# Expert bias rows and their selector as 128-row matmul operands instead of 40-row ones

## What is computed

```python
xf = _layernorm(x.reshape(-1, Dd), ln_g, ln_b)
logits = xf @ router_w
scores, idx = jax.lax.top_k(logits, K)          # K = 2 of E = 8 experts
gate = jax.nn.softmax(scores, axis=-1)
# one expert:
x = _layernorm(x, g, b)
x1 = x @ W1 + b1
x2 = jnp.clip(x @ W2 + b2, -20.0, 20.0)
hidden = jnp.clip(x1 * (x2 * jax.nn.sigmoid(x2)), -10000.0, 10000.0)
return jnp.clip(hidden @ Wo + bo, -10000.0, 10000.0)
```

## Time and profile before

| | |
|---|---|
| median of 3 runs | 579.73 us |
| lowest, highest | 577.4 us, 579.78 us |
| span of the profiled execution | 574.8 us |
| mean granted TensorE clock | 0.954 of full speed |
| instructions | 6831 |
| TensorE matmuls, VectorE, ScalarE, GpSimd instructions | 2579, 669, 406, 143 |

### The profile page before, as it was taken

The page is one execution under the profiler, slowest core; times in us unless marked ns, Lnnn a source line. Parts: engine busy times, 40 slices in busy tenths (PEclk is TensorE's granted clock), DMA queues, the critical chain, the costliest instruction groups (busy, mean ns, idle before and its releaser), DMA issues.

```text
span 574.8 us, 6831 instructions
## 1 busy us (share of the span) xinstructions
PE 514.5 (89%) x2579; PEld 444.6 (77%) x2579; DVE 430.0 (75%) x669; ACT 280.2 (49%) x406; POOL 234.6 (41%) x143
## 2 busy tenths in 40 slices
PE   3899999999999998989988886579999999996994
PEld 3899889999999997878877674456777676674773
DVE  6558977734433345889997776866999999997996
ACT  3425313332332235767775013329669659647630
POOL 5000433333333411122226712323686696690762
PEclk9999999999999999889999979569999999998889
DMA  8289763343344331020016233574888988984632
GB/s 315 94 282 343 234 260 121 121 146 98 125 147 146 128 137 70 1 74 1 1 58 210 114 111 109 196 285 175 328 322 310 388 313 324 391 298 180 220 110 111
DMA packets 20929, 106.32 MB, mean 185 GB/s; under 512 B 4720, under 2 KB 5104, under 8 KB 11168
## 3 DMA queue, kind: packets, MB, share of 16 engines
q1 hardware_dynamic: 15328, 91.53, 42.7%
q0 software_dynamic: 3696, 7.96, 4.2%
q10 hardware_dynamic: 1872, 6.39, 3.6%
HBM read 98.96 MB, written 6.91 MB: 184 GB/s over the span
## 4 chain that ended last, share of the span: by engine, by line
PE 52%; DVE 28%; issue 8%; ACT 5%; POOL 4%; DMA 1%; DVEq 0%; ACTq 0%; POOLq 0%
PE ps L1115 46%; DVE lo L728 11%; DVE sg L1031 4%; PE ps L1178 3%; POOL xres L480 2%; PE ps L1218 1%; ACT hi L561 1%; DVE xres L1047 1%; ACT xg L645 1%; DVE y L1001 1%; DVE hh L1038 1%; DVE x2c L1027 1%; DVE xg_lo L988 1%; DVE ht_lo L993 1%; ACT sg L654 1%
## 5 line engine op out<-in xcount | busy, mean ns | idle before, releaser
L728 DVE TENSOR_TENSOR lo<-raw,hi 128x2048 fp32r<-128x2048 f32 x58 | 153.8, 2668 | 54.8 <-ACT hi L561 54.6
L561 ACT ACTIVATE hi<-raw 128x2048 fp32r<-128x2048 f32 x70 | 131.8, 1913 | 77.0 <-PE ps L1115 65.0
L447 POOL DMA_INDIRECT mask_rows<-colf,bits x48 | 55.9, 1164 | 134.7 <-DMA mask_rows<-colf,bits 82.1
L489 POOL TENSOR_TENSOR lo<-raw,hi 128x2048 fp32r<-128x2048 f32 x12 | 64.9, 5408 | 50.5 <-ACT hi L561 50.4
L1115 PE MATMUL ps<-xt_hi,hi 128*128 128x384 f32 x192 | 65.2, 340 | 2.2 <-DVE xt_lo L744 2.2
L1115 PE MATMUL ps<-xt_lo,hi 128*128 128x384 f32 x192 | 65.1, 339 | 0.0
L1115 PE MATMUL ps<-xt_hi,lo 128*128 128x384 f32 x192 | 64.9, 338 | 0.0
L1115 PE MATMUL ps<-hi,xg_hi 128*128 128x512 f32 x128 | 54.3, 425 | 7.2 <-DVE lo L728 5.7
L1115 PE MATMUL ps<-lo,xg_hi 128*128 128x512 f32 x128 | 52.3, 409 | 0.0
L1115 PE MATMUL ps<-hi,xg_lo 128*128 128x512 f32 x128 | 52.2, 408 | 0.0
L455 POOL TENSOR_SCALAR pr<-pr,small 128x384 f32<-128x384 f32 x16 | 19.9, 1246 | 75.0 <-DVE small L853 75.0
(11 more groups left out here) (209 smaller groups left out, 1131.1 us busy)
## 6 DMA issues: line engine op xcount, KB each, us to landing
raw<-in_wf SPq DMA_DIRECT2D x42, 1024.0 KB, 6.3
raw<-in_wg SPq DMA_DIRECT2D x28, 1024.0 KB, 5.5
xfb<-in_wf SPq DMA_DIRECT2D x6, 1024.0 KB, 5.8
src_i<-in_srcb ACTq DMA_DIRECT2D x4, 768.0 KB, 6.2
dst_i<-in_dstb ACTq DMA_DIRECT2D x4, 768.0 KB, 9.0
y_rows<-y SPq DMA_DIRECT2D x6, 512.0 KB, 2.9
xin<-in_x SPq DMA_DIRECT2D x3, 512.0 KB, 4.4
xres<-in_x SPq DMA_DIRECT2D x3, 512.0 KB, 4.2
```

The source lines that it names most:

```text
L447: pool.indirect_dma_start(out=mbuf[:, :], out_offset=bass.IndirectOffsetOnAxis(ap=bits[:, 1, g:g + 1], axis=0), in_=colf[:, 5, g:g + 1], i ...
L489: pool.tensor_tensor(lo[SLOT[c]][:, :], raws[RAW[c]], f32(hi[SLOT[c]][:, :]), ALU.subtract).then_inc(pool_lo_done, 1)
L561: act.activation(hi[SLOT[c]][:, :], raws[RAW[c]], ACT.Copy).then_inc(hi_done, 1)
L728: dve.tensor_tensor(lo[SLOT[c]][:, :], raws[RAW[c]], f32(hi[SLOT[c]][:, :]), ALU.subtract).then_inc(lo_done, 1)
```

## The change

`brow_f`, `brow`, `sels` and `selx` get 128 rows in place of 48. The clearing of `brow_f` and `sels`, the rounding of `brow_f` into `brow` and the setting of `selx` run over 128 rows. The bias matmuls read all 128 rows of both operands. Rows 48 to 127 are zero. The loads, the low parts in rows 32 to 47 and the order of every engine's instructions stay.

```diff
@@ -185,12 +185,12 @@
             with ExitStack() as rowbuild:
-                brow_f = sb(rowbuild, "brow_f", [48, 2 * D], F32)
+                brow_f = sb(rowbuild, "brow_f", [P, 2 * D], F32)
...
-            brow = sb(ffn, "brow", [48, 2 * D], F32R)
+            brow = sb(ffn, "brow", [P, 2 * D], F32R)
...
-            sels = sb(ffn, "sels", [48, NE], F32)
-            selx = sb(ffn, "selx", [48, 3, P], F32R)
+            sels = sb(ffn, "sels", [P, NE], F32)
+            selx = sb(ffn, "selx", [P, 3, P], F32R)
@@ -500,7 +500,7 @@
-                pool.tensor_copy(selx[:, slot, :], sels[:, e:e + 1].to_broadcast([48, P])).then_inc(sel_set, 1)
+                pool.tensor_copy(selx[:, slot, :], sels[:, e:e + 1].to_broadcast([P, P])).then_inc(sel_set, 1)
@@ -1077,7 +1077,7 @@
-                dve.tensor_copy(selx[:, 0, :], sels[:, bass.ds(e, 1)].to_broadcast([48, P])).then_inc(over_sel, 1)
+                dve.tensor_copy(selx[:, 0, :], sels[:, bass.ds(e, 1)].to_broadcast([P, P])).then_inc(over_sel, 1)
@@ -1262,7 +1262,7 @@
-                pe.matmul(bank, selx[0:40, e % 3, :], brow[0:40, cols], start=True, stop=False)
+                pe.matmul(bank, selx[:, e % 3, :], brow[:, cols], start=True, stop=False)
@@ -1277,7 +1277,7 @@
-                    pe.matmul(B[3 + part], selx[0:40, e % 3, :], brow[0:40, cols], start=True, stop=False)
+                    pe.matmul(B[3 + part], selx[:, e % 3, :], brow[:, cols], start=True, stop=False)
@@ -1341,7 +1341,7 @@
-                pe.matmul(bank, selx[0:40, 0, :], brow[0:40, bias_cols], start=True, stop=False)
+                pe.matmul(bank, selx[:, 0, :], brow[:, bias_cols], start=True, stop=False)
```

## The result

| | before | changed |
|---|---|---|
| median of 16 runs | 578.31 us | 575.1 us |
| span of the profiled execution | 574.8 us | 572.2 us |
| mean granted TensorE clock there | 0.954 | 0.945 |

The ratio is 0.9947, with a 95% interval of 0.9928 to 0.9966: faster by 0.5%. The forecast was 579.4 us and no measurable change, in a range that began at 576.6. (The kernel before measured 578.31 over 16 runs, not the 579.73 of the first three.) Two of the sixteen runs before took 998.96 and 1952.44 us; without them the median is 578.08.

A forecast was written before the change was run, and what follows sets the result against it. VectorE was taken to set a period of 21.78 us an expert, with TensorE's slack inside it. The span of 574.8 less 0.30 for expert 0 is 574.5, with 4.9 around it 579.4 us; range 576.6 to 580.9.

The forecast's parts named there:

- By columns: 0: Selector L503 on GpSimd: its time goes with columns, so 128 rows add 0; by rows it would be +0.48 us each.
- in experts 2 to 6, nothing: TensorE's relief there saves no time at the end, since VectorE doesn't wait for TensorE.
- The 128-row bias matmul at 0.23 us: Bias matmul on TensorE: 0.23 us to the next start, the rate of 128-row neighbours, in place of 0.42.
- The relief of 0.40 for a `down` pair: TensorE saves 0.40 us on each of eight `down` bias pairs, 3.2 us in all.
- After transposes: TensorE saves 0.30 us on an `up` bias matmul behind the transposes: 0.46 in place of 0.76.
- Expert 0, -0.30: VectorE waits for TensorE before the hidden tile of expert 0; 0.30 us gained at the end, bounds 0 and 0.89.
- Setup, 0: Clearing `brow_f` and rounding it over 128 rows add 0; bounds by rows +3.0 and +5.7 us.
- the two rules of the Trainium skill: Few rows don't shorten a matmul (rival: no relief, 579.7 us, chance 0.10); against it, changing tiling mode drains the engine.
- The relief: Rival: all 7.7 us that TensorE saves reach the end, 572.0 us; chance 0.12, partly for a partial gain.
- GpSimd's time: Rival: GpSimd's clearing and the selectors of experts 3 to 7 go by rows, +5.4 us, 585.1 us; chance 0.05.
- The clock: Rival: more TensorE idleness lowers its clock through the last `down`, +2.5 us, 582.2 us; chance 0.05.
- The base: Starting time of the forecast: median 579.73 us of three runs, 4.9 us above the profiled span of 574.8.

## Why the prediction was wrong

**The step that failed** is a sentence in "What the change adds": the selector L503 was priced by how long it takes itself, "By columns: 0". That was right for its own time (288 and 295 ns at the least, 2349 and 2348 in the middle) and it missed what its rows decide: which engine is served next. The term was given bounds of 0 and +0.48 us each, and nothing below zero, with no reason that excluded a gain. It was -4.6 us, once, in VectorE's pair of splits, and 3 to 4.5 us less time: 0.9923 with that one selector over 128 rows in the kernel before, 0.9995 with it alone back at 48 in the changed kernel.

The trace of before had the row: a pair of splits of 11.86 us at 507.78, among pairs of 7.3 us. I read one expert of the steady ones and took it for all; "in experts 2 to 6, nothing" was said with the waits of VectorE, and the waits don't show it, because an engine that is held up inside an instruction counts as busy. In the prediction I described the two engines as excluding each other (at 402.86 us), and didn't ask of each GpSimd instruction that changes whether it stands at such a handover.

**The steps that held.** The 128-row bias matmul at 0.23 us: yes in a `down` pair, 0.32 behind transposes. The relief of 0.40 for a `down` pair: 0.39. After transposes: 0.30 forecast, 0.39 measured. Only 0.21 of it lies where I looked; the other 0.18 is the later start that the 40-row bias matmul also had. Expert 0, -0.30: -0.39 between the kernels that differ in this and in the selectors. Setup, 0: 1801 and 1811 ns, 3416 and 3420 ns. The period, unchanged: 21.75 to 21.78 us over experts 2 to 6. VectorE's wait from 0.89 to 0.6: 0.51. The gap before the second chunk of `down`, about 0.7 us: 0.86. The reason for the bound was right, and so was the worth of the matmuls: the kernel with them alone measured 0.9995.

**The rivals.** Of the two rules of the Trainium skill, the one of "TensorEngine Tiling (Array Packing)", Key Properties, fits: the loss goes with the rows, and the kernel with 128-row selectors and 40-row matmuls keeps it. The Trainium skill's rule in "TensorE: Matmul & The Clock Gate" (LDWEIGHTS, and what matters for a kernel) is not contradicted for the matmul in itself (the bias matmuls of L1265 last 494 ns in the middle with 40 rows and 478 with 128, their weight loads 183 and 190), but it doesn't cover what a change of shape costs its neighbours. The relief didn't reach the end (0.9995 with the matmuls alone). GpSimd's time didn't go by rows (1801 and 1811 ns). The clock: it didn't stay low through the last `down`. It fell after 2.0 us of TensorE's idleness ahead of that `down`, and the matmuls from L1317 on were slow until 553.87 us, when starts were 0.23 us apart again. The cost was near 0.6 us where I had 2.5.

**The base.** I put 4.9 us around the span; it is 1.8. The base of the forecast, 579.7 us, was the median of three runs and lay 1.4 us above that of sixteen. The range began at the lowest run less 0.8; with 576.65, the lowest of the sixteen, it would have begun near 575.9, still above the result. (Its upper end, by the terms that I gave, is 579.78 + 1.25 = 581.0, not 580.9.)

**Still open.** The changed kernel measured 0.9947, the kernels with the selector alone 0.9918 and 0.9923, in different sets of runs. The intervals of the first two overlap between 0.9928 and 0.9937. Whether the 128-row matmuls take back a little, through longer idle time and a lower clock, isn't settled. The profiled executions don't show it: the changed kernel and the one with 40-row matmuls reach the clearing at 309.84 and 309.78 us and have spans of 572.2 and 572.3. Nor do the kernels without the gain, which measured 0.9995 with 128-row matmuls. But the sixteen runs of the changed kernel reach from 572.22 to 577.63 us, wider than any other kernel of this study (the two long executions of the kernel before aside), and why is open.

## What to carry to other kernels

Where VectorE and GpSimd keep each other out, ask of every short GpSimd instruction what runs right behind it: here one that left the last sixteen rows without work let the next long one take the other engine's turn. A wait for its completion, or full rows, gave VectorE its turn back at no cost that showed. And look for instances of a group that are longer than their siblings: a mean over 31 splits hides one that was held up twice, and no list of waits names it. When one engine's operations take twice as long as the other's and they share a resource, try all of them on the faster one: here this gave 2.3%, and moving only one of two lost 1.7% or gained 1.7%, depending on which.

## What the runs showed of the hardware that I had not expected

- VectorE's splits (two operands in SBUF) and GpSimd's splits and selectors are served in turn, a whole instruction at a time; 2.2 and 4.6 us are the turns of the splits. VectorE's reads from PSUM (L993, L1001, L1037) run beside GpSimd's split: 0.69, 1.22 and 0.69 us, as without it. L1038, with one operand, in SBUF, doesn't: 0.43 us alone, 4.02 at 545.66 us in the kernel before, beside a split of GpSimd from 544.66 to 549.40.
- GpSimd's turn isn't tied to one instruction: with 48 or 112 rows in the first, the second follows in the same turn; with 120 or 128 it doesn't. A wait for completion has the effect of full rows.
- 40-row matmuls of 512 columns among 128-row ones cost 0.39 us more than 128-row ones, as a pair among matmuls and likewise as a single one behind transposes: this points to the change of rows as what costs, more than to each such matmul.
